# Conditioned residual convolutions in fp32r: small products, evacuations and splits of the first sample placed anew

## What is computed

```python
x = x + L0(x)   # grouped conv, 4 groups, 9 taps, padding 4, plus cond @ c_weight.T and a bias
x = x + L1(x)   # out = sum_k att[k] * weight[k] @ x, plus att @ bias_k: a mix of 8 matrices per sample
x = x + L2(x)   # the same with its own weights
x = x + L3(x)   # grouped conv as in L0
```

## Time and profile before

| what | value |
|---|---|
| median of three runs | 674.84 us (674.57 to 676.61) |
| the profiled execution | 675.46 us |
| its span, first to last instruction | 673.7 us |
| PE busy | 651.5 us, 97% of the span |
| DVE, ACT, POOL busy | 76%, 39%, 36% |
| mean granted clock | 0.995 |

### The profile page before, as it was taken

How to read it: one execution, slowest core, us unless ns; L and a number is a source line. 1 busy time by engine, 2 the same in 40 slices (tenths; PEclk the granted TensorE clock), 3 DMA queues, 4 the chain that set the end, 5 groups by cost and what they waited for, 6 DMA issues and landing times.

```text
span 673.7 us, 24614 instructions
## 1 busy us (share of the span) xinstructions
PE 651.5 (97%) x11200; PEld 630.1 (94%) x11200; DVE 510.7 (76%) x945; ACT 262.8 (39%) x323; POOL 243.1 (36%) x91
## 2 busy tenths in 40 slices
PE   4989999999999999999999999999999999999994
PEld 3679888999999999999999999999999999999994
DVE  5699778788778777777877777787877787788736
ACT  5432443333443343343334234334324433433435
POOL 5022432324443333444243344334244433334220
PEclk9999999999999999999999999999999999999998
DMA  7137888998888899888889888889988888987646
GB/s 234 69 101 159 196 192 176 176 180 184 197 194 192 153 210 163 195 198 195 186 154 218 158 194 196 192 167 183 186 180 198 191 191 152 212 158 145 132 105 157
DMA packets 50181, 118.24 MB, mean 176 GB/s; under 512 B 5541, under 2 KB 26074, under 8 KB 42330
## 3 DMA queue, kind: packets, MB, share of 16 engines
q1 hardware_dynamic: 49586, 116.95, 81.0%
q10 hardware_dynamic: 360, 0.69, 0.5%
q0 software_dynamic: 192, 0.02, 0.0%
HBM read 35.33 MB, written 33.55 MB: 102 GB/s over the span
## 4 chain that ended last, share of the span: by engine, by line
PE 94%; DVE 2%; DMA 2%; ACT 1%; issue 1%; ACTq 0%; SPq 0%; DVEq 0%
PE ps L829 79%; PE ps L896 13%; DMA out_planes<-out_taps 1%; DMA out_sb<-in_L_cond_weight 1%; PE ps L883 1%; ACT out_sb L537 1%; DVE x_lo L598 1%; DVE y_lo L606 0%; ACT x_hi L559 0%; PE ps L929 0%; DVE acc L645 0%; DVE mat L645 0%; PE ps L922 0%; ACT out_taps L485 0%; PE ps L995 0%
## 5 line engine op out<-in xcount | busy, mean ns | idle before, releaser
L399 POOL COPY out_sb<-out_planes 128x2048 f32<-128x2048 f32 x30 | 117.4, 3915 | 283.3 <-DMA out_planes<-out_taps 283.3
L467 ACT ACTIVATE y_hi<-ps,bias_tab 128x512 fp32r<-128x512 f32 x128 | 77.5, 689 | 188.9 <-PE ps L829 185.0
L393 POOL COPY x_planes<-x_in 128x2048 f32<-128x2048 f32 x29 | 113.0, 3896 | 90.5 <-DVE x_lo L598 90.5
L616 DVE SCALAR_TENSOR_TENSOR z_lo<-ps,bias_tab,z_hi 128x1024 fp32r<-128x1024 f32 x62 | 76.7, 1279 | 59.7 <-ACT z_hi L477 59.7
L606 DVE SCALAR_TENSOR_TENSOR y_lo<-ps,bias_tab,y_hi 128x512 fp32r<-128x512 f32 x128 | 87.3, 746 | 38.7 <-ACT y_hi L467 38.6
L829 PE MATMUL ps<-z_hi,taps_lo 32*128 32x512 f32 x1488 | 104.2, 398 | 1.0 <-issue 1.0
L829 PE MATMUL ps<-x_hi,taps_hi 32*128 32x512 f32 x1536 | 103.2, 399 | 1.0 <-ACT x_hi L559 0.7
L829 PE MATMUL ps<-x_hi,taps_lo 32*128 32x512 f32 x1536 | 101.3, 392 | 0.0
L829 PE MATMUL ps<-x_lo,taps_hi 32*128 32x512 f32 x1536 | 100.5, 390 | 0.0
L896 PE MATMUL ps<-y_hi,mix_w 32*128 32x512 f32 x1024 | 99.3, 390 | 0.9 <-DVE y_lo L606 0.9
L829 PE MATMUL ps<-z_lo,taps_hi 32*128 32x512 f32 x1488 | 97.7, 390 | 0.1
(11 more groups left out here) (118 smaller groups left out, 619.2 us busy)
## 6 DMA issues: line engine op xcount, KB each, us to landing
x_in<-in_x SPq DMA_DIRECT2D x31, 1024.0 KB, 11.5
out_planes<-out_taps SPq DMA_DIRECT2D x122, 256.0 KB, 8.5
out<-out_sb SPq DMA_DIRECT2D x30, 1024.0 KB, 4.2
mix_w<-prod SPq DMA_DIRECT2D x128, 128.0 KB, 4.6
x_in<-in_x SPq DMA_DIRECT2D x2, 512.0 KB, 5.0
out<-x_planes SPq DMA_DIRECT2D x8, 128.0 KB, 2.2
out_taps<-in_L_cond_weight SPq DMA_DIRECT2D x1, 512.0 KB, 5.1
mix_w<-in_L_cond_weight SPq DMA_DIRECT2D x1, 512.0 KB, 6.4
```

What stands on the lines that cost most here:

```text
L393: pool.tensor_copy(x_planes[:, :, :], planes(x_in[t.par(d)], slice(0, S))).then_inc(x_planed, 1)
L399: pool.tensor_copy(out_sb[t.par(d)][:, :].rearrange("c (s p) -> c p s", p=PH), out_planes[:, :, :])\
L467: act.activation(y_hi[:, g, :], ps[:, bank(t, 0) + g, :], ACT.Identity, bias=bias_tab[:, b, g:g + 1]).then_inc(y_hi_done, 1)
L616: dve.scalar_tensor_tensor(out=z_home(t, 0)[1][:, 2 * h:2 * h + 2, 1:S + 1], in0=ps[:, k:k + 2, :], scalar=bias_tab[:, b, 2 * G:BIAS], in1 ...
```

## The change

All of it lies before the third sample.

- **TensorE**: the context transposes go ahead of the first turn of `conv0(zero)`; `contexts` and `logits` follow `hidden(1)` at once; the transposes of `mix2`, the attention's transpose, the spread of the attention (table) and `conv_biases` come after turns 5 and 6 of sample 0 instead of 12 to 28; `agg` is made for layer 1 alone. The remaining 30 turns follow: 9, the product, 8, then ten times one turn and one small product of `mixed_bias(k)`. These are the 8 from before and two of `bias_k` with the attention (8 rows), which put the two layers' `agg` into the same PSUM sum; three turns close. `mix(zero)` stands after 14 turns of sample 1 instead of 22.
- **ScalarE** takes over the attention's transpose, both copies into `bias_tab`, `agg` and the mix's bias; the split of sample 1 (`high_x1`) is in two halves; `taps_high(1, ...)` comes after the exponentials.
- **VectorE**: `ctx_columns` ahead of the softmax; the low parts of samples 0 and 1 in pieces of two phases (`low_direct`) around the matrices; three of the four `taps_low(1, ...)` after them; the second piece of sample 1 after `low_y(zero)`.
- **GpSimd** zeroes no `bias_tab`, and its first half of sample 2's planes waits for `low_y`'s first piece; SP's load of sample 2 waits, as before, for sample 0's low part, which is now done later.

```diff
 ACT
             gelus(0)
+            act.wait_ge(ctxT_psum, 2)
+            for l in range(2):
+                act.activation(ctxT[l], ps[:, 7, 128 * l:128 * l + 128], ACT.Copy).then_inc(ctxT_done, 1)
             gelus(1)
...
             mix2_transposed(0)
+            act.wait_ge(attT_psum, 1)
+            act.activation(attT_sb[:, :, :], ps[0:K, 6, 256:320]...).then_inc(attT_done, 1)
+            for p in range(PH):
+                taps_high(1, p)
+            act.wait_ge(bias_psum, 1)
+            for l in range(2):
+                act.activation(bias_tab[:, :, G * l:G * l + G], ps[:, 7, ...], ACT.Copy).then_inc(bias_tab_done, 1)
             mix2_transposed(1)
+            high_x1(0)
+            act.wait_ge(agg_psum, 1)
+            act.activation(agg[:, :], ps[:, 6, 320:320 + N], ACT.Copy).then_inc(agg_done, 1)
+            high_x1(1)
             zero = Step(0, 0)
-            high_x(zero, 1)
-            act.wait_ge(bias_tab_done, 2)
+            act.wait_ge(mixed_psum, 1)
+            act.activation(bias_tab[:, 0:N, 2 * G], ps[:, 5, 0:N], ACT.Copy).then_inc(bias_tab_done, 1)
             high_y(zero)
 DVE
+            low_direct(0, half(1), slice(0, 2), False)
             dve.wait_ge(taps_zeroed, 8)
-            for p in range(PH):
-                taps_low(1, p)
+            taps_low(1, 0)
             dve.wait_ge(att_tab_psum, 1)
             dve.tensor_copy(att_tab[:, :, :], ...).then_inc(att_tab_done, 1)
...
             mix_matrices(zero, 0)
+            low_direct(0, half(1), slice(2, PH), True)
+            split_product(zero, 0)
             dve.wait_ge(agg_done, 1)
             dve.tensor_tensor(out=mixed_terms, ...).then_inc(mixed_step, 1)
-            split_product(zero, 0)
...
-            low_x(zero, 1)
-            dve.wait_ge(bias_tab_done, 3)
+            for p in range(1, PH):
+                taps_low(1, p)
+            dve.wait_ge(x_hi_done, 2)
+            low_direct(1, slice(0, S), slice(0, 2), False)
+            dve.wait_ge(bias_tab_done, 2)
             low_y(zero)
+            low_direct(1, slice(0, S), slice(2, PH), True)
             mix_matrices(zero, 1)
 PE
+            def mixed_bias(k):
+                if k == 0:
+                    pe.wait_ge(mixed_step, 1)
...
+                w, a = (mix2_wT[:, k, :], mixed_terms[:, k, :]) if k < K else (bias_k[k - K], attT_sb[:, k - K, :])
+                last = pe.matmul(ps[:, 5, 0:N], w, a, start=(k == 0), stop=(k == MIXED - 1))
...
+            conv0(zero, range(6, SHIFTS))
+            pe.wait_ge(taps_lo_done[0], PH)
+            conv0(zero, range(SHIFTS, 15))
+            pe.wait_ge(bias_tab_done, 2)
             product(zero, 0)
-            conv0(zero, range(32, TURNS))
-            mixed_bias()
+            conv0(zero, range(15, 23))
+            for k in range(MIXED):
+                conv0(zero, range(23 + k, 24 + k))
+                mixed_bias(k)
+            conv0(zero, range(23 + MIXED, TURNS))
 
             pe.wait_ge(bias_tab_done, 3)
             pe.wait_ge(prod_summed, 1)
-            conv0(first, range(22))
+            conv0(first, range(14))
             mix(zero)
-            conv0(first, range(22, TURNS))
+            conv0(first, range(14, TURNS))
```

More of the change, by code:

```diff
@@ L46 @@
 BIAS = 2 * G + 1
+MIXED = K + 2
 PLANED = 2
@@ L453, in high_x, with high_x1 @@
                 b, p = t.i + d, t.par(d)
[L454 to L461, removed]
+                act.wait_ge(x_planed, b + 1 - PLANED)
+                act.wait_ge(conv0_done, G * (b - 1))
+                act.activation(x_hi[p][:, :, 1:S + 1], x_planes[:, :, :], ACT.Copy).then_inc(x_hi_done, 1)
+            def high_x1(h):
+                act.wait_ge(x_loaded[1], DMA)
+                last = act.activation(x_hi[1][:, :, 1 + half(h).start:1 + half(h).stop], planes(x_in[1], half(h)),
+                                      ACT.Copy)
+                if h == 1:
+                    last.then_inc(x_hi_done, 1)
             def high_y(t):
@@ L596, in low_x, with low_direct @@
                 dve.wait_ge(x_hi_done, b + 1)
-                direct = isinstance(b, int) and b < PLANED
-                dve.tensor_tensor(out=x_lo[p][:, :, 1:S + 1],
-                                  in0=planes(x_in[p], slice(0, S)) if direct else x_planes[:, :, :],
+                dve.tensor_tensor(out=x_lo[p][:, :, 1:S + 1], in0=x_planes[:, :, :],
                                   in1=x_hi[p][:, :, 1:S + 1].bitcast(F32), op=ALU.subtract).then_inc(x_lo_done, 1)
+            def low_direct(b, s, p, done):
+                last = dve.tensor_tensor(out=x_lo[b][:, p, 1 + s.start:1 + s.stop], in0=planes(x_in[b], s)[:, p, :],
+                                         in1=x_hi[b][:, p, 1 + s.start:1 + s.stop].bitcast(F32), op=ALU.subtract)
+                if done:
+                    last.then_inc(x_lo_done, 1)
             def low_y(t):
@@ L726, in second @@
                 low_z(t)
[L728 to L733, removed]
             def ctx_columns(l):
@@ L975, in _ @@
             hidden(0)
-            pe.wait_ge(taps_hi_done[0], PH)
-            conv0(zero, range(3))
-            hidden(1)
-            conv0(zero, range(3, 8))
-            logits()
-            conv0(zero, range(8, SHIFTS))
             for l in range(2):
@@ L985, in _ @@
             last.then_inc(ctxT_psum, 2)
+            pe.wait_ge(taps_hi_done[0], PH)
+            conv0(zero, range(3))
+            hidden(1)
+            contexts()
+            logits()
+            conv0(zero, range(3, 5))
             mix2_transposes(0)
-            pe.wait_ge(taps_lo_done[0], PH)
-            conv0(zero, range(SHIFTS, 16))
             pe.wait_ge(att_step, 4)
@@ L992, in _ @@
             last.then_inc(attT_psum, 1)
+            conv0(zero, range(5, 6))
             pe.wait_ge(spread_done, 1)
```

82 lines of the change are left out of this document (25 added, 57 removed).

## The result

The changed kernel takes **679.56 us** (median of 20 runs, 675.65 to 681.67) where the kernel before, on the same chip, takes 675.27 (20 runs, 673.93 to 677.0). The ratio is 1.0047, 95% interval 1.0034 to 1.0059: slower by over 0.3%, where 674.5 was forecast, a range to 676.0, and slower had a chance of 0.05. The 20 runs fall into two groups: 9 of 675.65 to 677.71 us at a mean granted clock of 0.992 to 0.996, and 11 of 679.23 to 681.67 at 0.988 to 0.990. That is the first hint of where to look. Six of the nine have 0.996 and a median of 676.2; the eleven have a median of 680.3, so within this one kernel a low clock goes with 4.1 us. A mean clock lower by 0.008 is, over 676 us, 5.4 us of full rate, or 10.8 us at the half.

What follows compares the result with a forecast made beforehand. TensorE's queue was taken as the bound. Less waiting (-0.27, -0.38, -0.6), interleaving (+2.3), `bias_k` (+0.3), level and run changes (+1.85, -3.0, -0.5) gave -0.3 us: 675.2 profiled, 674.5 median, range 672.8 to 676.0.

Steps and rivals of the forecast that it cites:

- a step of turn and product: At the mixed-bias interleaving: each turn with one small product takes 0.77 us; eight products cost 4.3 against 1.97 in one block.
- If the level rises at 21.9 again: TensorE's early queue: clock level rises at 21.9 us as before, leaving two turns below it; turn 9 starts at 22.05.
- Line 995's successor (now line 996) at 17.2, 2.0 long: Early small product on TensorE: starts at 17.2 us and takes 2.0 wholly at the lower level, against 1.27 before.
- rival 3: TensorE's start: level rises later because turns are rare early; +1.4 us, 675.9, or 677 if near 28; chance 0.16.
- A wait of 0.55 at the product: At the first product: TensorE arrives at 23.75, VectorE's matrices allow it at 24.3; the 0.82 wait shrinks to 0.55.
- Terms at 26.4, no wait at line 931; bias wait gone: Mixed bias: VectorE's terms ready at 26.4, before the first small product at 26.96; the 0.38 us bias wait goes.
- Sample 1's first turn at 34.55: After the tenth small product and three turns: sample 1 starts at 34.55 us, 0.6 later than the 33.97 before.
- A wait of 0.3 at the first mix, at 38.2: First mix, after 14 turns of sample 1: TensorE arrives at 37.9 us and waits 0.3 until 38.2.
- The mix moved up is worth 0.6: First mix after 14 turns instead of 22: the 0.91 us wait for `y_lo` falls to 0.3, counted as -0.6.
- Rival 1: Interleaved products: their weight loads hide under the turns; eight save 2.5 us, time 672.0; chance 0.12.
- Rival 2: TensorE's start: level rises at 18 to 20 us instead of 21.9; -0.8 to -1.3 us, 673.5; chance 0.15.
- rival 4: Waits at product and mix all go, matrices come 0.55 us sooner, pairs cost 0.1 less each; 672.8; chance 0.07.

Runs made afterwards that it cites:

- the joined version: Changed kernel with first product and the ten small products in one stretch after turn 27, VectorE's terms ahead of its split, mix after 16 turns; 673.21 us, ratio 0.9955.
- the one in twos: Changed kernel with two turns and two small products alternating five times, instead of one and one ten times; 675.61 us, ratio 0.9977.

## Why the prediction was wrong

**The step that failed** is "a step of turn and product is 0.23 + 0.34 + 0.20 = 0.77 us. Eight such products cost 8 x 0.54 = 4.3", together with what stands ahead of it: that TensorE runs at its lower level for a stretch after its first turn "and at the upper afterwards". The size is right: 27.62, 28.39, 29.16 and so on to 33.02 is 0.77 a step, eight times. What is wrong is that the level was taken as a thing that rises once. The order of the work itself took it away again. Within the changed kernel the runs with the long fall stand 4.1 us above those without. Undoing the order alone gave back 0.9%, 6.1 us, of which 2.3 was in the sum; making the same order in the kernel before cost 6.6 us over the same products in a block. No rival had this. It is not the whole miss: the six runs at 0.996 have no such fall, and their median of 676.2 still stands 1.7 above the 674.5. Of that, 0.4 is the base (the kernel before has 675.27 in 20 runs, and the forecast starts from 674.84). For the rest a second step is at hand, "If the level rises at 21.9 again" (below): at 24.2, the mean of ten profiles, a late rise costs 1.2 by an estimate, half of 2.3.

**The rest of the sum came out right in total, and in part by luck.** Without the alternation it read -0.3 - 2.3 = -2.6 us, or -0.38%. The kernel without it measured -0.44% (-0.66 to -0.22); its profile has `conv3` 1.9 earlier than before, and a span shorter by 2.0. But the sum lets the level rise at 21.9 in both kernels, and it rose at 20.4 in the mean of one family and at 24.2 in that of the other: 1.9 us that the sum lacks, and no run shows what made up for them. Point by point, in the profile:

- *Line 995's successor (now line 996) at 17.2, 2.0 long*: 17.66 and 2.04. The first turn was 0.27 later than taken (10.37), since `x_hi` was.
- *The level rises again at 21.9*: it did not. By pace, 21 matmuls of turns took from 22.09 to 23.82, 1.73 us, where the upper level gives 1.2, so it changed near 23.1. This is **rival 3's mechanism, at a part of its size**. And the profile of before had misled me: of its family (kernels that are the same up to 24 us) it rose latest. This row of the kernel with eight single products stands where the earlier trace rows have 2.08 for 16:

```profile
19.39 1.38 PE L829 MATMUL ps<-x_hi,taps_lo 32*128 32x512 f32 x16
```

  The six profiles of that family rose at 19.8 to 21.9 (mean 20.4), ten of the changed one's at 22.9 to 26.4 (mean 24.2). So 3.7 us later, about half of it lost, as an estimate from the two paces. One execution of one kernel was no base for a time that varies by 2 us. That the scarce turns are the reason is what four turns moved up show, in one profile: 18.97, against 23.7, 24.5 and 24.4 in three without.
- *A wait of 0.55 at the product*: none. TensorE came at 24.91 and the matrices ended at 24.76. Being later at the lower level used up the wait, as rival 3 said.
- *Terms at 26.4, no wait at line 931; bias wait gone*: right.
- *Sample 1's first turn at 34.55*: 35.83. Of the 1.28, 0.66 was there at 27.62 (later start, later rise) and 0.62 came in the fall from 33.4.
- *A wait of 0.3 at the first mix, at 38.2*: 0.28, at 40.31. From the mix to `conv3` 9.12 were measured and 9.1 forecast, with the wait of 0.52 in it, so `conv3` came at 49.43 instead of 47.3.
- *The mix moved up is worth 0.6*: the wait went, but with the mix after 22 turns the time can't be told from it.
- *Rival 1* (loads hide, pairs 0.45 apart) fell at the first pair. 0.45 is what 32 rows give. *Rival 2* and *rival 4* did not occur: the level rose later, and the `y_lo` wait stayed at 0.28.

The median lies above the profiled execution because the fall has several lengths, 3.4 us in this one and 10.2 in that on the other chip. Eleven of the 20 runs have the clock of the long one.

What do the clocks of the other kernels say? The kernel before had no run under 0.992 in 107; the block after turn 33, the joined version, the one in twos and the one with four single products had none under 0.994 in 66. But the kernel before had 43 of its 107 at 0.992 or 0.993, and so had 3 of 12 with the eight in a block, 3 of 12 with 32 rows, 9 of 12 with `y_lo` moved, and 4 of 12 with the block after turn 36. Profiles without a fall have means of 0.994 to 0.996, and 3.4 us at the half take 0.0025 off, so these runs probably had a short fall. All of these last kernels have a block with the wait for the bias behind it; the 66 have none. That is argued from the means: of these kernels only that of `y_lo` moved shows the fall in its profile. What it costs isn't clear either: those 43 runs have the same median as the other 64 (676.4 and 676.3).

**Open.** What drops the level at one place and not at another. Four single products did it in the kernel before and not in the changed one, where six turns followed at once. A block with a wait beside it did it in two profiled executions (34.4 and 29.2) and did not in the earlier trace rows, which has the same block and the same wait. Nor does the clock explain every long run: 12 of the 107 runs of the kernel before took 678.0 to 682.5 us at 0.994 to 0.997. The runs show what raises the risk, not a limit.

## What to carry over

Price small matmuls by their neighbours: at the upper level one of 128 rows, alone among turns, cost 0.54 us here, one in a block 0.23 to 0.25, and one of 32 rows, alone, 0.22. When a change spreads small work between large, look at the granted clock behind it, not only at gaps, and look at the clocks of all runs, and at those of the kernel before too: the kernel with 1.8 us less waiting ahead of its first mix was 0.5% slower. **Keep small products together, directly behind one another, with full turns on both sides and no wait; that version, the joined one, beats the kernel before in three sets of runs (0.9955, 0.9949, 0.9951), and the changed one in the set that has both (1.0032 against 0.9949).**

## What the runs showed of the hardware

- **A TensorE busy without a gap can be set back to its lower level.** Alternating 0.23 us of turns with single fp32 products of 128 rows was followed by a granted clock of 0.50 for 3.4, 6.8 and 10.2 us, with PE busy for all of it. In four profiled executions it began 1.8 to 5.8 us after the first single product. Four such products in the changed kernel did not do it.
- **The fall may last beyond its cause.** In the kernel with four single products full turns ran behind them from 28.12, still at 0.50, and the level came back only at 33.5.
- **The first rise is not at a fixed time of the kernel.** It came between 18.97 and 26.4 us by how early turns ran and from one execution to the next by 2 us. In the windows view the clock's column is 1.00 ahead of it. The times given here are those at which the trace's own record of the clock begins, and the pace of equal rows agrees with them.
- **The busy share of the weight loads says little here.** It is 94% of the span before and 82% after, yet three profiles of the joined kernel have 94, 84 and 93% at spans of 670.9, 672.0 and 672.4. From the entry of the loop over the samples (134.34 in the kernel before, 136.79 in the changed one) to the end both take the same, 539.4 and 539.1 us:

```profile
136.79 1.19 PE L826 MATMUL ps<-z_hi,taps_lo 32*128 32x512 f32 x13 [1.06 <-issue]
```
